# Hosted projection tiles moved from odd to even head pairs in a cross-attention kernel, with the context splits moved to pairs 4 and 6

## What is computed

```python
q = split_heads(hidden @ w_q, 20)
k, v = split_heads(text @ w_k, 20), split_heads(text @ w_v, 20)
out_text = merge_heads(softmax(q k^T / 4) v)
k_ip, v_ip = split_heads(ip_h @ w_k_ip, 20), split_heads(ip_h @ w_v_ip, 20)
out_ip = merge_heads(softmax(q k_ip^T / 4 + mask_ip) v_ip)
out = (out_text + out_ip) @ w_out + b_out + hidden
```

## Time and profile before

| | before |
|---|---|
| median of 3 runs | 508.35 us (507.78 to 509.81) |
| profiled execution | 508.77 us, of which 506.9 us is the span from first to last instruction |
| mean granted TensorE clock | 0.976 of full speed |
| busy share: TensorE / VectorE / ScalarE / GpSimd | 92% / 77% / 54% / 30% |
| shares of the chain that ended last | TensorE 66%, VectorE 14%, issue 7%, DMA 7%, ScalarE 3% |

### The profile page before, as it was taken

One profiled execution on the slowest core, in us unless ns is written; L12 is line 12 of the kernel. 1 busy time (PEld: TensorE's weight loads), 2 busy tenths in 40 slices (PEclk: granted clock), 3 DMA queues, 4 the chain that ended last, 5 costly groups with the idle time before them and its releaser, 6 DMA issues.

```text
span 506.9 us, 11023 instructions
## 1 busy us (share of the span) xinstructions
PE 465.9 (92%) x4250; PEld 319.7 (63%) x4250; DVE 391.2 (77%) x705; ACT 275.3 (54%) x357; POOL 154.1 (30%) x242
## 2 busy tenths in 40 slices
PE   2899486999999999999999999999999998889987
PEld 2698364676666766676667766676667765555543
DVE  3824484796978789697978789697978788999933
ACT  3733022565646476456645566556645555666672
POOL 4490010313304152313204142323204141533442
PEclk9989695999999999999999999999999999999999
DMA  8989996929486585929495675939495655483021
GB/s 270 292 219 232 328 290 188 318 66 306 135 257 205 148 259 162 328 75 319 132 276 185 188 239 151 328 79 308 131 283 180 194 181 156 156 263 87 7 58 53
DMA packets 96453, 101.80 MB, mean 201 GB/s; under 512 B 16896, under 2 KB 83504, under 8 KB 96400
## 3 DMA queue, kind: packets, MB, share of 16 engines
q1 hardware_dynamic: 95408, 98.92, 63.1%
q0 software_dynamic: 992, 2.17, 2.0%
HBM read 67.87 MB, written 33.23 MB: 199 GB/s over the span
## 4 chain that ended last, share of the span: by engine, by line
PE 66%; DVE 14%; issue 7%; DMA 7%; ACT 3%; SPq 2%; POOL 1%; POOLq 0%; ACTq 0%
PE pv L819 15%; PE pj L828 10%; PE score_t L804 10%; PE score_q L743 6%; DVE max_cols L595 5%; PE score_q L694 4%; PE score_q L689 3%; PE score_q L695 3%; PE score_q L691 3%; PE score_q L696 3%; PE score_q L690 3%; PE score_q L698 2%; DVE qk_out L587 2%; PE score_q L699 2%; DMA v_rows<-v_out 1%
## 5 line engine op out<-in xcount | busy, mean ns | idle before, releaser
L520 ACT ACTIVATE probs<-score_t 128x1024 f32<-128x1024 f32 x155 | 158.3, 1021 | 139.5 <-PE score_t L804 139.2
L595 DVE TENSOR_REDUCE max_cols<-score_q 128x4 fp32r<-128x992 f32 x155 | 183.1, 1181 | 65.4 <-PE score_q L743 64.8
L819 PE MATMUL pv<-probs,v_cur 128*32 128x256 f32 x1920 | 120.2, 383 | 2.2 <-ACT probs L520 2.1
L434 POOL TENSOR_TENSOR o_turned<-o_turned,inv_cols 128x256 f32<-128x256 f32 x80 | 53.9, 674 | 158.0 <-DVE inv_cols L645 157.9
L819 PEld LDWEIGHTS pv<-probs,v_cur 128*32 128x32 f32 x1920 | 54.6, 109 | 40.6 <-issue 3.2
L426 POOL TENSOR_TENSOR x_all<-x_all,bias_sb 128x640 f32<-128x640 f32 x16 | 25.0, 1564 | 137.6 <-DMA x_all<-in_x 137.6
L828 PE MATMUL pj<-wo_sb,o_all 128*128 128x320 f32 x186 | 63.2, 460 | 4.0 <-DVE o_all L650 3.9
L512 ACT ACTIVATE o_all<-pv 128x512 f32<-128x512 f32 x80 | 47.8, 598 | 30.0 <-PE pv L819 29.3
L642 DVE STREAM_TRANSPOSE o_turned<-o_all 128x512 f32<-128x512 f32 x80 | 55.5, 693 | 10.9 <-ACT o_all L512 10.9
L804 PE MATMUL score_t<-q_stack,k_stack 64*128 64x256 f32 x420 | 52.9, 330 | 7.3 <-ACT probs L520 5.9
L804 PEld LDWEIGHTS score_t<-q_stack,k_stack 64*128 64x128 f32 x420 | 31.6, 186 | 44.3 <-issue 35.7
(11 more groups left out here) (163 smaller groups left out, 683.3 us busy)
## 6 DMA issues: line engine op xcount, KB each, us to landing
k_stack<-k_parts SPq DMA_DIRECT2D x33, 320.0 KB, 5.0
q_stack<-q_parts SPq DMA_DIRECT2D x33, 320.0 KB, 5.5
q_parts<-qk_out SPq DMA_DIRECT2D x32, 256.0 KB, 4.7
k_parts<-qk_out SPq DMA_DIRECT2D x32, 248.0 KB, 5.2
raw<-in_ctxT SPq DMA_DIRECT2D x14, 512.0 KB, 4.5
v_rows<-v_out SPq DMA_DIRECT2D x32, 160.0 KB, 5.0
v_stage<-v_rows SPq DMA_DIRECT2D x16, 320.0 KB, 6.2
x_all<-in_x SPq DMA_DIRECT2D x16, 320.0 KB, 6.1
```

Source lines behind the costliest of these rows:

```text
L434: pool.tensor_tensor(out, out, inv_cols[:, n % SLOTS, :].unsqueeze(2).broadcast_to([P, 2 * S // 32, DH]), ALU.mult).then_inc(scaled, 1)
L520: nc.scalar.activation(probs[:, slot(t % 2, p), :], key_bank(t, p), ACT.Exp, scale=SCALE)\
L595: nc.vector.tensor_reduce(out=max_cols[:, h, :, at:at + 4:2].rearrange("p t e -> p e t"), in_=both[:, :, :, 0:TEXT], op=ALU.max, axis=AX.X ...
L819: last = mm(pv[32 * t:32 * t + 32, at:at + S], values_of(u, kind, 4 * k + t), probs[:, slot(u, 2 * k + t // 2), a:a + S], start=kind != 1, ...
```

## The change

A hosted tile is issued in even pairs, behind P times V, and no longer in odd pairs, behind the scores and the output products; with this the first tile of a batch comes in pair 0 rather than pair 1. Its copy on ScalarE and its low part on VectorE follow in the next odd pair, so they move from even to odd pairs. The high part of the context is made in pairs 4 and 6 (before 5 and 8), its low part in pairs 5 and 7 (before 6 and 9). The number of instructions and their shapes stay, and so do the order on the SP and GpSimd queues.

```diff
         def tile_due(t, p):
-            if p % 2:
-                return None
-            n = 5 * (t + 4) + p // 2 - 1
-            return n if (hosted(t) if p else hosted(t - 1)) else None
+            return 5 * (t + 4) + p // 2 if p % 2 and hosted(t) else None
...
-                    if hosted(t) and p % 2:
+                    if hosted(t) and p % 2 == 0:
                         tile(5 * (t + 4) + p // 2)
...
-SPLIT_C_HI, SPLIT_C_LO = {5: 0, 8: 1}, {6: 0, 9: 1}
+SPLIT_C_HI, SPLIT_C_LO = {4: 0, 6: 1}, {5: 0, 7: 1}
```

## The result

| | before | after |
|---|---|---|
| median of 4 runs | 508.06 us (506.56 to 509.81) | 578.53 us (576.7 to 579.56) |
| span of the profiled execution | 506.9 us | 577.0 us |
| mean granted TensorE clock | 0.976 | 0.947 |

The ratio is 1.138, with a 95% interval of 1.134 to 1.143. The page of after, its head and the granted clock in 40 slices.

What follows compares the result with a forecast made beforehand. TensorE's own work in its order was taken as the bound, with waits covered by that order. Terms A to E, 31.4 + 4.2 + 3.6 + 24.5 + 5.5 = 69.2, on 508.8 gave 578.0 us, range 557 to 593.

Steps and rivals of the forecast that it cites:

- D: Context's second half, one shared buffer: its late load and VectorE's split delay pair 8, 4.9 us in five odd batches, 24.5.
- E: TensorE's 5 us idle before pair 8 drops its clock to the low level: 1.1 us per splitting odd batch, 5.5.
- A: Odd pairs lose the tile that covers waits for maxima and exponentials: 2.37 us per even batch, 2.86 per odd, 31.4 in all.
- B: Seam between P times V and the tile behind it: 0.07 us at each of 60 tiles, 4.2, ends 0 and 10.8.
- C: Start: VectorE's split in pair 7 delays batch 0's first key scores to about 85.1; 3.6 us, ends 0 and 6.
- pairs 3 and 9: nothing: Odd pairs 3 and 9 have 1.19 and 1.78 us of output products, covering the 1.15 opened, so no loss.
- the nearest row: An output product beside a tile, about 0.59 us, of which up to 0.18 was taken as possible seam.
- the clock stays up: Rival: one 5 us idle stretch before pair 8 is too short to lower TensorE's clock; 572.5 us, chance 0.22.
- faster: Rival: evacuations spread more evenly, `turn_back` no longer late, and odd pairs don't wait; 506 us, chance 0.02.
- does nothing: Rival: copies and tiles keep their distance and TensorE's sum of work is the same; 508.8 us, chance 0.03.
- the load is hidden anyway: Rival: the context's second half lands by the time ScalarE wants it; 548 us, chance 0.12.
- dearer: Rival: the context load lands later (30 us) or the seam behind P times V costs 10.8; 590 us, chance 0.11.

Runs made afterwards that it cites:

- tiles_only: The changed kernel with tiles in even pairs, but the context's splits back in pairs 5 and 8 (high), 6 and 9 (low): 544.0 us, ratio 1.070.
- kept_warm: The changed kernel with 16 matmuls of no use in the idle time between pairs 7 and 8 of five odd batches: 572.76 us, ratio 1.126.
- load_ahead_of_rows: The kernel before with the new splits alone, and on SP the second half's load moved ahead of the row maxima's write and read-back: 519.94 us, ratio 1.023.

## Why the prediction was right, step by step

The time came out as the forecast case had it, 578.53 for 578.0. D was right in mechanism and close in size, and so was E, though its size had no working behind it. A was right in mechanism and 7.6 us too small; B (4.2), D (1.6) and C (0.4) were too large, batch 12 gave 0.6 back, and so most of it cancelled. The chains of A, C, D and E are what the prediction had right; that their sum came within 1 us is luck.

**A, the cover.** The mechanism holds: in bare pairs key scores are 1.62 apart and query scores 1.78, for 1.82 predicted. In the batches the prediction had 31.4 less the 1.15 before the third key scores of batch 0, so 30.2; measured, with B at nothing (below), are 5.1 in batch 0, 14.5 in the even batches, 14.6 in the odd ones (by the run of the tiles alone) and 3.6 in batch 11: 37.8. Two sub-steps failed. The larger is batch 0, for which the sum had 1.2: no batch stands before it, so it has no output products, and pairs 3, 5 and 9 are bare there too, as the 1.62 from 98.41 to 100.03 shows. The other is "pairs 3 and 9: nothing" and the price of a wait as chain less work. In batch 2 pairs 1, 3, 5, 7 and 9 cost 1.20, 0.23, 0.17, 1.22 and 0.04 us, with the slower start of the pair behind counted in; the sum had 1.15, 0, 0.07, 1.15 and 0. Behind a wait, key and query scores are released one after the other, 0.50 apart for 0.34, and P times V comes 0.43 behind for 0.33: of the 1.22 us, 0.95 is the pair (1.62 less 0.67), and 0.27 lies in the next one. In batch 11, which has no split, the sum had 2.86 for the 3.6 measured; in the five odd batches that split it had 2.86 for 2.9, but only because these already took 0.5 or more longer than batch 11 before the change.

**B, the seam.** In after a tile starts 1.43 behind P times V (205.55 to 206.98); in before key scores did so after 1.44 (206.34 to 207.78). The row of before, then the first weight load of the tile in after (PEld):

```profile
206.34 1.50 PE L819 MATMUL pv<-probs,v_cur 128*32 128x256 f32 x24
```
```profile
206.98 0.19 PEld L691 LDWEIGHTS score_q<-x_hi,wq_hl 128*128 128x128 f32 x1 [0.41 <-issue]
```

The seam is nothing, and 4.2 us of the sum were wrong. The rule of the Trainium skill that was weighed there, page "TensorE: Matmul & The Clock Gate", section "Step-by-step: what each phase is for", gave the right time, against the value taken from the nearest row. That the load was pulled ahead is not shown: in the trace the tile's first weight load starts at 206.98, where its matmul's row starts too, and only the loads behind it start ahead of their matmuls. The 0.59 of that nearest row is no seam: in after an output product takes 0.60 where no tile stands behind it (pair 9, from 220.80 to the next key scores at 222.61, three products).

**C, the start.** First key scores at 86.12 for 85.1, third at 93.06 for 93.4, so 4.4 late for 4.75. The chain was right; the size is two misses that cancel. The first key scores came 1.0 later than computed, since the load itself went out later (75.35 for 74.41 in before) and ScalarE made the high part at 80.08 for 78.94. From there to the third it took 6.94 for the 8.3 computed with a tile wholly at the low clock: the granted clock was 1.00 again from 90 to 92 us, before that tile ended at 91.44.

**D, the second half.** Every link came where the working put it, counted from the query scores of pair 5 (203.26): load issued at 4.46 (4.6), high part at 8.94 (9.1), key scores of pair 8 at 10.96 (11.25). With the clock kept up it costs 4.57 per odd batch for 4.9: 1.16 on VectorE (1.1), and 3.41 for the load (3.8).

**E, the clock.** 1.11 per odd batch for 1.1. Behind idle stretches of 4.2 to 4.6 us the granted clock was at the low level, 0.50, in all five batches, as forecast. That the size fits is luck: the prediction "put" the 1.1 without a sum for it. The rival "the clock stays up" had 572.5 us, and the run that keeps it up has 572.76.

**Batch 12** gave 0.6 back, which no term had: in before its second query scores stood idle for 1.08 us, with no releaser that the trace names; after has no idle time in front of that row. It goes with the tiles' place: batch 12 takes 20.34 in tiles_only and kept_warm too, and 20.91 in load_ahead_of_rows. In before, VectorE's low part of the last tile ends at 423.03 and those query scores start at 423.13, so the wait for that evacuation is the likely cause; no run was made to test it.

Of the rivals, "faster" and "does nothing" fell to the waits that the earlier trace rows had shown in batches without tiles, and "the load is hidden anyway" to the 4.48 us in front of ScalarE's high part; "dearer" needed a seam that isn't there and a D of 30 us, which is 22.9 by the above.

## What to carry to other kernels

Work that is to be moved may be the cover of a wait: list for each slot the chains that run beside it, and price the slot that is emptied, in the first and last rounds too, where what else fills it differs. When two engines' chains end close to each other, the trace can name one of them alone: here shortening the one it named gave nothing in the even batches. A load that waits for a buffer has its price in the queue ahead of it as well: in the kernel with the splits alone, one issue moved ahead of another's wait on SP gave 22.8 us back.

## What the runs showed of the hardware

VectorE's low part of the context took 1.52 us at 216.55 in after, but 1.16 at 206.53. Beside the slow one GpSimd has these rows:

```profile
216.37 0.62 POOL L431 TENSOR_TENSOR o_turned<-o_turned,inv_cols 128x256 f32<-128x256 f32 x1 [6.88 <-DVE inv_cols L642]
217.07 1.32 POOL L436 TENSOR_TENSOR o_all<-o_turned 128x128 f32<-128x128 f32 x1
```

The first ends at 216.99, and VectorE's row is 0.36 longer than usual; the second takes 0.46 elsewhere (208.24 in the same trace) and here ends at 218.39, 0.32 behind VectorE's end. Beside the fast one, GpSimd's first row took 1.48 rather than 0.62. That looks like taking turns, whoever is first running through. The Trainium skill, page "SBUF — State Buffer", section "SBUF: two separate sides", describes this for a VectorE operation with two SBUF inputs against a GpSimd operation that reads SBUF, as an exclusive lock; these rows agree, and no run was made to test it. It is some 0.36 of the 1.16 that VectorE adds to D.

The granted clock was 0.50 behind all five waits of 4.2 to 4.6 us in after, and in the same place in load_ahead_of_rows it went both ways: 1.00 behind waits of 1.95, 2.00 and 2.16 us, 0.50 behind 2.08 and 2.10. The length of the last wait alone did not decide it there; the two that fell also had 0.4 us of idle time one tile earlier. Whether that is the cause was not tested.
